# Two small-head attentions: where the inverse of the softmax sums, the row copies and the bf16 split subtractions are made

## The reference

```
q = q * cos + _rotate_half(q) * sin          # k likewise; 16 heads, d = 8, S = 2048
scores = einsum('bhqd,bhkd->bhqk', q, k) * d ** -0.5      # layer 1: causal mask
attn = softmax(scores, axis=-1)
out = einsum('bhqk,bhkd->bhqd', attn, v)
```

## Time and profile before

| what | value |
|---|---|
| median of three runs | 2145.32 us (2144.81 to 2145.73) |
| span of the profiled execution, first to last instruction | 2143.6 us |
| median less this span, taken for what lies around it | 1.7 us |
| busy: TensorE, VectorE, ScalarE, GpSimd | 1853.8, 1599.2, 1374.3, 314.9 us |
| a0: first exponential to last OD copy | 110.0 to 722.4 us |
| a1: first projection about, first exponential, last OD copy | 1533, 1617.5, 2002.9 us |

### The profile page before, as it was taken

One profiled execution on the slowest core, in us unless ns is written; L12 is line 12 of the kernel. 1 busy time (PEld: TensorE's weight loads), 2 busy tenths in 40 slices (PEclk: granted clock), 3 DMA queues, 4 the chain that ended last, 5 costly groups with the idle time before them and its releaser, 6 DMA issues. The chain is left out here.

```text
span 2143.6 us, 40610 instructions
## 1 busy us (share of the span) xinstructions
PE 1853.8 (86%) x16064; PEld 920.6 (43%) x16064; DVE 1599.2 (75%) x2327; ACT 1374.3 (64%) x2546; POOL 314.9 (15%) x464
## 2 busy tenths in 40 slices
PE   6799999989999669849989999999668998998585
PEld 2122222222222249824766776777412332334385
DVE  6899999999995343445777777877588989786324
ACT  3489989989888433434555556566246987877331
POOL 2000000000000160432431221211110000000123
PEclk7589999999999869968999999999888999999788
DMA  5000000000000149600000000000100000000084
GB/s 163 1 4 4 7 5 4 7 4 5 5 4 7 43 146 309 230 17 1 1 1 1 1 1 1 1 1 1 51 1 2 7 5 7 7 7 11 12 281 155
DMA packets 51356, 81.36 MB, mean 38 GB/s; under 512 B 7520, under 2 KB 36192, under 8 KB 51040
## 3 DMA queue, kind: packets, MB, share of 16 engines
q1 hardware_dynamic: 46000, 70.30, 10.4%
q0 software_dynamic: 3072, 6.30, 0.9%
q10 hardware_dynamic: 2096, 2.17, 0.4%
HBM read 62.49 MB, written 11.67 MB: 35 GB/s over the span
## 5 line engine op out<-in xcount | busy, mean ns | idle before, releaser
L633 DVE TENSOR_REDUCE a_mx<-psum 128x2 f32<-128x1024 f32 (+2 forms) x832 | 908.8, 1153 | 70.6 <-PE psum L434 45.5
L567 ACT ACTIVATE a_cs<-psum 128x512 f32<-128x512 f32 (+3 forms) x1664 | 858.3, 572 | 125.8 <-PE psum L454 79.5
L479 PE MATMUL psum<-a_cs,a_V 128*16 128x256 f32 (+1 forms) x6400 | 505.9, 387 | 12.0 <-ACT a_OD L544 9.5
L434 PE MATMUL psum<-a_KS,a_QS 48*128 48x512 bf16 (+3 forms) x1664 | 326.1, 386 | 61.2 <-DVE a_mx L633 59.4
L454 PE MATMUL psum<-a_QS,a_KS 51*128 51x512 bf16 (+3 forms) x1664 | 337.6, 381 | 6.9 <-ACT a_cs L567 3.8
L1767 PE MATMUL psum<-b_VW,b_ST 128*128 128x129 f32 x2176 | 251.6, 277 | 13.0 <-DVE X L1877 13.0
L1767 PEld LDWEIGHTS psum<-b_VW,b_ST 128*128 128x128 f32 x2176 | 247.5, 193 | 14.7 <-DVE X L1877 14.7
L454 PEld LDWEIGHTS psum<-a_QS,a_KS 51*128 51x128 bf16 x1664 | 87.2, 93 | 364.4 <-ACT a_cs L567 320.7
L1748 PE MATMUL psum<-b_GT,AT 128*128 128x512 f32 (+3 forms) x640 | 242.0, 532 | 1.6 <-ACT b_ST L1803 1.6
L479 PEld LDWEIGHTS psum<-a_cs,a_V 128*16 128x16 f32 x6400 | 107.5, 94 | 261.7 <-issue 125.5
L1852 DVE TENSOR_TENSOR b_M<-b_M,b_ST 128x512 f32<-128x512 f32 (+3 forms) x288 | 174.9, 607 | 41.9 <-ACT b_ST L1803 12.1
(11 more groups left out here) (213 smaller groups left out, 1533.5 us busy)
## 6 DMA issues: line engine op xcount, KB each, us to landing
e_W<-in_l_experts SPq DMA_DIRECT2D x46, 576.0 KB, 5.2
e_W<-in_l_experts SPq DMA_DIRECT2D x22, 768.0 KB, 4.9
yg<-e_yout SPq DMA_DIRECT2D x14, 256.0 KB, 5.9
xg<-zeros SPq DMA_DIRECT2D x2, 1472.0 KB, 9.5
a_cs<-in_rope ACTq DMA_DIRECT2D x4, 512.0 KB, 8.8
a_QS<-a_mrow SPq DMA_DIRECT2D x128, 3.0 KB
a_num<-a_OD SPq DMA_DIRECT2D x128, 16.0 KB
a_den<-a_OD SPq DMA_DIRECT2D x128, 16.0 KB
```

The source lines that it names most:

```text
L434: mm = pe.matmul(ps[:, 2 * slot + half, 0:width], QS[rows, 2 * p + i, q_cols(qb, qt * P, P)], KS[rows, 2 * p + i, c * BLK:c * BLK + width] ...
L479: mm = pe.matmul(ps[32 * j:32 * j + 2 * HD, AV_BANK, a:b], V[:, kt, HPP * p + j, :], probs(e, a, b), start=(kt == 0 and half == 0), stop=last,
L567: act.activation(probs(e, c, BLK), ps[:, S_BANK + e % S_SLOTS, c:BLK], ACT.Exp, scale=scale).then_inc(exp_done, 1)
L633: dve.tensor_reduce(mx[:, pk % 2, qt, 2 * i:2 * i + 2, c], banks, AX.X, ALU.max).then_inc(max_done, 1)
```

## The change

It has four parts, all in `small_head_stage` and its planner. (1) For the first three blocks the sums go to DRAM: `gather` moves one row for each head into `sums`; `spread_sums` reads them back as `denc` (128x64, each partition with its own 64 queries); VectorE inverts these only (`invert`); `spread_inverse` writes them to DRAM, waits for that, and issues 16 DMAs that broadcast each head's row over its 8 partitions of `rden`; GpSimd multiplies. The fourth block keeps the old way. `FINISH` becomes 5. (2) The turns of packs 1 to 15 leave the ring of the maxima and take a place in the ring of banks 4 to 6, and ScalarE copies them to `mrow` (L627's work). (3) The eight `split_rest` and eight `split_low` of each attention move from VectorE to GpSimd. (4) Waits are adapted.

```diff
@@ TensorE, max_item @@
+                    if item in plan.place_of:
+                        wait_bank(pe, item)
+                        turn(item[1], plan.bank(item)).then_inc(s_ready, 1)
+                        return
...
@@ SyncE, gather and after @@
-                        for dst, r in ((num, 32 * j), (den, 32 * j + HD)):
-                            sp.dma_start(dst[h:h + HD, :], OD[r:r + HD, p, :]).then_inc(gathered[p], 16)
+                        sp.dma_start(num[h:h + HD, :], OD[32 * j:32 * j + HD, p, :]).then_inc(gathered[p], 16)
+                        r = 32 * j + HD
+                        if k < NB - 1:
+                            row = k * HEADS + HPP * p + j
+                            sp.dma_start(sums[row:row + 1, :], OD[r:r + 1, p, :]).then_inc(gathered[p], 16)
+                        else:
+                            sp.dma_start(den[h:h + HD, :], OD[r:r + HD, p, :]).then_inc(gathered[p], 16)
+                def spread_sums(k):
+                    for p in range(NPACK):
+                        sp.wait_ge(gathered[p], 16 * 2 * HPP * (k + 1))
+                    if k:
+                        sp.wait_ge(inverse_ready, k)
+                    sp.dma_start(denc[:, :], sums[k * HEADS:(k + 1) * HEADS, :].rearrange("h (c q) -> (h c) q", c=HD)).then_inc(sums_in, 16)
+                def spread_inverse(k):
+                    mine = inverse[k * HEADS:(k + 1) * HEADS, :]
+                    sp.wait_ge(inverse_ready, k + 1)
+                    sp.dma_start(mine.rearrange("h (c q) -> (h c) q", c=HD), rdenc[:, :]).then_inc(inverse_out, 16)
+                    sp.wait_ge(inverse_out, 16 * (k + 1))
+                    if k:
+                        sp.wait_ge(finished, k)
+                    for h in range(HEADS):
+                        sp.dma_start(rden[h * HD:(h + 1) * HD, :],
+                                     mine[h:h + 1, :].broadcast_to([HD, BLK])).then_inc(inverse_in, 16)
+                todo += [(plan.first[NPACK * (k + 1)] + 2, 2, k) for k in range(NB - 1)]
+                todo += [(plan.first[NPACK * (k + 1)] + FINISH + 0.2, 3, k) for k in range(NB - 1)]
...
@@ GpSimd @@
+                rotate(0)
+                pool.memset(V[:, :, :, HD:], 1.0).then_inc(ones_set, 1)
+                for s in range(NOP):
+                    split_rest(s)
+                    if s + 1 < NOP:
+                        rotate(s + 1)
+                    split_low(s)
...
                     pool.wait_ge(split_done, pk + 1)
+                    for k in range(NB - 1):
+                        if pk == (NPK - 1 if causal and k == NB - 2 else NPACK * (k + 1) + 1):
+                            for p in range(NPACK):
+                                pool.wait_ge(gathered[p], 16 * 2 * HPP * (k + 1))
+                            pool.wait_ge(inverse_in, 16 * HEADS * (k + 1))
+                            pool.tensor_tensor(OT[:, q_cols(order[k], 0, BLK)], num[:, :], rden[:, :], ALU.mult).then_inc(finished, 1)
...
@@ ScalarE @@
+                def row_copy(pk):
+                    entry = ("turn", pk)
+                    act.wait_ge(s_ready, plan.place_of[entry] + 1)
+                    if pk >= 2:
+                        wait_shift(act, pk - 2)
+                    act.activation(mrow[:, pk % 2, :], ps[0:TR, plan.bank(entry), :], ACT.Copy).then_inc(row_ready, 1)
...
@@ VectorE @@
+                def invert(k):
+                    dve.wait_ge(sums_in, 16 * (k + 1))
+                    if k:
+                        dve.wait_ge(inverse_out, 16 * k)
+                    dve.reciprocal(rdenc[:, :], denc[:, :]).then_inc(inverse_ready, 1)
```

More of the change, by code:

```diff
@@ L147, in __init__ @@
                 self.ring += mine
-        self.ring += self.items[self.sent(-1):]
+        self.ring += [item for item in self.items[self.sent(-1):] if item[0] == "scores"]
         self.number = {}
@@ L156, in __init__, with bank @@
             count += item[0] == "scores"
+        self.halves = []
+        for row in self.rows:
+            cut = (len(row) + 1) // 2
+            self.halves += [row[:cut], row[cut:]]
+        self.entries = []
+        for u, row in enumerate(self.halves):
+            self.entries += [("exp", HPP * (u // 2) + 2 * (u % 2) + half) for half in range(2)]
+            self.entries += [item for item in row if item[0] == "turn"]
+        self.place_of = {entry: n for n, entry in enumerate(self.entries)}
+    def bank(self, entry):
+        return S_BANK + self.place_of[entry] % S_SLOTS
     def lay(self, ahead):
@@ L251, in small_head_stage @@
         mrow = sb("mrow", [TR, 2, BLK], BF16)
+        denc, rdenc = sb("denc", [P, BLK // HD]), sb("rdenc", [P, BLK // HD])
+        sums, inverse = (nc.dram_tensor(f"{tag}_{n}", ((NB - 1) * HEADS, BLK), F32, kind="Internal").ap()
+                         for n in ("sums", "inverse"))
         tokens_in = sem("tokens_in")
@@ L332, in _, with rotate, split_rest, split_low @@
                     opening.gpsimd(pool)
-                for s in range(NOP):
+                def rotate(s):
                     u = s % 2
[L335 to L338, removed]
                     pool.wait_ge(turned, 2 * (s + 1))
                     pool.tensor_tensor(t1[:, u, :], t1[:, u, :], t2[:, u, :], ALU.add).then_inc(rot, 1)
+                def split_rest(s):
+                    u = s % 2
+                    pool.wait_ge(hi, s + 1)
+                    pool.tensor_tensor(t2[:, u, :], t1[:, u, :], terms[:, u, 0, :], ALU.subtract).then_inc(rest, 1)
+                def split_low(s):
+                    u = s % 2
+                    pool.wait_ge(mid, s + 1)
+                    pool.tensor_tensor(terms[:, u, 2, :], t2[:, u, :], terms[:, u, 1, :], ALU.subtract).then_inc(low, 1)
+                rotate(0)
+                pool.memset(V[:, :, :, HD:], 1.0).then_inc(ones_set, 1)
+                if opening:
+                    pool.memset(opening.zeros[:, :], 0.0).then_inc(opening.zeroed, 1)
+                for s in range(NOP):
[3 more added lines that the diff above has]
+                    split_low(s)
                 pool.wait_ge(ones_set, 1)
@@ L412, in mask, with turn @@
                                 mm.then_inc(ready, 1)
+                def turn(pk, bank):
+                    if opening and pk == 0:
+                        pe.wait_ge(opening.cast, 4)
+                    pe.wait_ge(split_done, pk + 1)
+                    for qt in range(TPB):
+                        mm = pe.matmul(ps[0:TR, bank, qt * P:(qt + 1) * P],
+                                       mterm[:, pk % 2, qt, :, :].rearrange("p h t -> p (h t)"),
+                                       core.identb[:, :], start=True, stop=True)
+                    return mm
                 def max_item(item):
+                    if item in plan.place_of:
+                        wait_bank(pe, item)
+                        turn(item[1], plan.bank(item)).then_inc(s_ready, 1)
+                        return
                     slot = slot_of(item)
                     if item[0] == "turn":
[L417 to L425, removed]
+                        turn(item[1], 2 * slot).then_inc(max_ready, 1)
                         return
@@ L508, in _ @@
                 for s in range(NS):
-                    row = plan.rows[s]
                     for half in range(2):
                         score(s, half)
-                        for item in row[half * (len(row) + 1) // 2:len(row) if half else (len(row) + 1) // 2]:
+                        for item in plan.halves[2 * s + half]:
                             max_item(item)
```

88 lines of the change are left out of this document (49 added, 39 removed).

## The result

The changed kernel takes 2123.72 us (median of four runs, 2122.35 to 2126.4) where the kernel before took 2145.53 us in four runs beside it: a ratio of 0.9903, with a 95% interval of 0.9889 to 0.9917. It is faster by 1%, some 21.8 us; I had forecast no change. Its profiled execution has a span of 2120.5 us, 23.1 us less than the one before.

A forecast was written before the change was run, and what follows sets the result against it. VectorE, busy 99.90 of 100 us in a0's body, was taken as the bound there. The terms summed to +1.4 us on 2143.6, 2145.0, plus 1.7 for the median: 2146.7 us, range 2134 to 2154.

The forecast's parts named there:

- low bound 0.48: SyncE's broadcasts: the lowest issue time allowed for each was 0.48 us, where 0.667 us was taken.
- the landing of the write: Inverse written to DRAM before the broadcasts: write and landing taken as 2.5 us, entered as 2.6 us in a1.
- Part 1 in a0: Three finishes of 5.45 us in a0 each become a covered inversion of 0.55 us: -14.7 us.
- the pipeline starting again: Finish in a0: the rest of its 5.45 us beyond VectorE's own 3.33 + 0.69 us of work.
- Part 2: Row copies at 30 pack changes: leaving VectorE gains nothing, the turn's new place costs 0.1 us each: +3.0 us.
- the bank order: Turn in the ring of three banks: next pair's second score waits for the second exponential, about 0.1 us a pack.
- Part 3: Subtractions moved to GpSimd in both leads: -2.2 us for each attention, -4.4 us together.
- operands 2 to 5 were hidden: Leads: subtractions for these operands cost nothing, as VectorE waits for the projection anyway; about three of 0.68 us count.
- Part 1 in a1: Work waiting behind the broadcasts in a1: +0.9 at k = 0, +6.5 at k = 1, +10.1 us at the end.
- three places: Waits in a1: first scores of pack 5 (+0.9), turn of pack 10 (+6.5), gathers 12 to 15 (+10.1 us).
- Sum: Whole kernel: -14.7 + 3.0 - 4.4 + 0.9 + 6.5 + 10.1 = +1.4 us on the profiled 2143.6 us.
- Broadcasts issue faster: Rival: SyncE issues broadcasts at 0.48 us each, 3.0 us less at each of three places in a1, 2137.7 us; chance 0.20.

The follow-up runs named there:

- p1_inverse: The kernel before with the compact inverse alone (sums through DRAM, broadcasts, FINISH 5, GpSimd's multiplications): ratio 0.9932 to the kernel before.
- p13_no_rows: The changed kernel with the turns back in the ring of the maxima and the row copies back on VectorE: ratio 0.9887 to the kernel before.
- ring_rows: The changed kernel with the turns back in the ring of the maxima, row copies still on ScalarE: 2120.55 us, ratio 0.9886 to the kernel before.
- p3_subs: The kernel before with only the sixteen split subtractions moved to GpSimd: ratio 0.9962 to the kernel before.
- spare_twice: The changed kernel with a second broadcast of each row into an unread tile, 32 broadcasts a block: ratio 0.9995 to the kernel before.
- late_old: p13_no_rows with a1's block k = 2 inverted the old way and GpSimd multiplying for k = 1 behind pack 10's split: ratio 0.9860 to the kernel before.
- changed_again: The changed kernel repeated without edits, on a chip like that of other follow-up runs: ratio 0.9910 to the kernel before.

## Why the prediction was wrong

The step that failed is "a gather DMA, also of 8 rows, takes 0.62 us, 0.667 with the gap; a load of 128 rows 0.43 us. I take 0.667 for the broadcasts, as they have 8 rows (low bound 0.48)". It chose its nearest row by the number of rows. The one that counts was where the two sides lie: the gathers have both in SBUF, the broadcasts read DRAM, and cost 0.335 us, half the value taken and under the low bound. With it went the landing of the write, 1.5 us after issue in a1 and not 2.6: I had it from a write of 256 KB, and this one has 32 KB. But the size isn't all of it. The same write took 2.76 us with its landing in the first block of a0, and 2.7 to 3.2 us there in every run that has it, 1.5 to 2.0 in the second block and 1.5 in the third; why was not tested. Point by point:

- **Part 1 in a0:** -14.7 us forecast, -14.7 measured; alone, in p1_inverse, -15.1. Right, as the finishes lay on VectorE's path. What the prediction called the pipeline starting again, 5.45 - 4.02 = 1.4 us, falls in some 6 us in which TensorE ran at half its clock (last section); no run parts the two, but the trace shows its matmuls slower there, not waiting.
- **Part 2:** +3.0 forecast, +4.4 measured against p13_no_rows (1.8 in a0, 2.6 in a1). In a0 right in mechanism, the bank order and not the copy, as ring_rows shows; in a1 some 1.1 us are the copy on ScalarE, which I had put at nothing. The gain of nothing on VectorE is right.
- **Part 3:** -4.4 forecast, -7.5 at the leads' ends in the trace after (3.4 and 4.1), -7.6 in p3_subs. Right in sign and too small. The step that fails is that operands 2 to 5 were hidden in a0: VectorE's second product of an operand comes 13.70 us after that of the operand ahead, where it was 14.10. The row of before, to the earlier trace rows, and the two of after:

```profile
37.52 0.74 DVE L586 SCALAR_TENSOR_TENSOR a_t<-psum,a_bkr,a_cs 128x512 f32<-128x512 f32 x1
```
```profile
36.42 0.75 DVE L690 SCALAR_TENSOR_TENSOR a_t<-psum,a_bkr,a_cs 128x512 f32<-128x512 f32 x1 [1.04 <-PE psum L459]
...
50.12 0.75 DVE L690 SCALAR_TENSOR_TENSOR a_t<-psum,a_bqr,a_cs 128x512 f32<-128x512 f32 x1 [1.03 <-PE psum L459]
```

  In a1 it is otherwise: the start of the lead gives 4.9 us (that product of operand 4 stands at 1531.36 for 1556.17, with 19.9 us from before a1 in it), and each later operand gives some 0.4 us of it back. The clock has little part in it (last section).
- **Part 1 in a1:** +17.5 forecast (0.9 + 6.5 + 10.1); measured, with packs 5 and 6, 9 to 11 and the end, -4.3 - 0.4 + 4.7 = 0.0. Right in its three places and wrong in size. 5.4 us at each are the broadcasts, and spare_twice, where they are given back, measures +1.3 + 5.1 + 10.0 = +16.4. A second misreading hides in it: for k = 1 I took pack 11 of before, 20.01 us, as undisturbed. It takes 18.52 us in late_old, pack 10 18.53, so the finish had cost 3.8 + 1.5 = 5.3 us and not 2.3.
- **Sum:** of the 24.5 us between forecast and profile (+1.4 and -23.1), 19.6 lie in a1, 1.0 in a0, 3.5 in the layers between, which is no effect, and 0.4 behind a1. In a1 17.5 are the three places behind the broadcasts, and 1.9 the lead.

The rival that came true is "Broadcasts issue faster". It named the right cause ("their source is DRAM") and stopped at 0.48 us, so at 2137.7 us; at 0.335 us, counted as that rival is, it gives 3 x 5.3 = 15.9 us off the forecast, 2130.8, and with the landing 2127.5. The range was cut at 2134 because of that low bound. The Trainium skill's rule on DMAs over fewer than 16 engines (DMA: Bandwidth & Descriptors, "Why a DMA increments its semaphore by 16 and not by 1") had been used to lean towards the dearer form. The runs don't bear that out as a price: eight rows from DRAM cost 0.30 us, the read of the sums from DRAM into 128 partitions 0.35, and 128 partitions within SBUF 0.55. The prediction's 0.62 against 0.43 had compared a DMA within SBUF with one from DRAM.

## What to carry to other kernels

Price a DMA's issue by a row with the same memories at both ends, then by its shape; and a landing by more than one row: the same write took 1.5 to 2.8 us in one trace. When a forecast is a difference of large terms that all hang on one price (here 16 issues at three places), that price is the range: bound it by every row that could be its like. A wait that is small on the trace is worth removing all the same: taking two of them away took 8.6 us from a1 (477.6 to 469.0), where the whole change had given 2.8. And look at the clock before taking the pack behind a disturbance as undisturbed.

## What the runs showed of the hardware

Beyond the prices of the issues (0.30 us from DRAM to 8 partitions, 0.335 with the gap; 0.65 within SBUF) there is the clock. The windows give busy time by engine, then the granted clock of TensorE as a share of 2.4 GHz. First, what a finish does in a0, in the kernel before: TensorE's first maximum behind it and one of 5 us later, then the clock of two stretches, ahead of the finish and behind it.

```profile
281.20 0.61 PE L434 MATMUL psum<-a_KS,a_QS 48*128 48x512 bf16 x2 [3.79 <-DVE a_mx L633]
...
286.61 0.38 PE L434 MATMUL psum<-a_KS,a_QS 48*128 48x512 bf16 x2
```
```profile
272.00:276.00 4.00, 4.00 (x48) 1.11 (x46) 4.00 (x5) 3.97 (x8) 0.00 (x0) 1.00 0.02 4
282.00:286.00 4.00, 4.00 (x28) 0.56 (x24) 2.88 (x4) 1.77 (x4) 0.00 (x0) 0.50 0.00 0
```

TensorE stood still for 3.79 us, waiting for VectorE. Then its clock is 0.50, the level of 1.2 GHz, from about 280 to 286 us, and the pair that takes 0.38 us at the upper level takes 0.61. Behind the finish of k = 1 in a1 it is at 0.50 up to 1914 us, some 4 us into pack 11, which is why that pack wasn't undisturbed. With the compact inverse alone (p1_inverse) the clock stays at 1.00 through the same block end. So a stop of TensorE costs more than its length: in spare_twice a wait of 3.57 us made pack 6 5.6 us longer.

Second, the lead of a0, in the kernel before and in the changed one:

```profile
40.00:90.00 50.00, 36.21 (x168) 7.99 (x168) 43.10 (x45) 19.06 (x22) 3.87 (x4) 0.60 0.00 1
```
```profile
40.00:90.00 50.00, 32.98 (x174) 8.07 (x166) 40.77 (x40) 21.00 (x24) 13.75 (x15) 0.75 0.00 1
```

0.60 against 0.75: between the levels of 1.2 and 2.4 GHz, the engine spent more of the 50 us at the upper one. p1_inverse, with the subtractions on VectorE, has 0.60 again; with them on GpSimd it is 0.74 in p3_subs, 0.72 in changed_again and 0.66 in p13_no_rows. In a1's lead it is 0.77 before and in p1_inverse, and with the subtractions on GpSimd 0.61, 0.69 and 0.77 (p3_subs, after, p13_no_rows). I had no term for it, and what sets it is open. It isn't what shortens the leads: in a1 these three end 116.9, 116.5 and 116.1 us from the first projection, 0.8 us apart for all of that difference in clock, where the two with the subtractions on VectorE, at 0.77, take 120.6 and 121.0.
